# Unread products in float32r instead of bf16 in layer 2's second edge pass

## The reference

```
for i in range(2):
    x1 = gat_layer(x1, src, dst, W[i], a_s[i], a_d[i], concat = (i == 0))
    x2 = gcn_layer(x2, src, dst, edge_weight, gcn_W[i])
out = maximum(x1, x2)
# gat: per head e = leaky_relu(es[src] + ed[dst]); att = softmax of e over the edges
#      of one dst; out = sum over edges of att * Wh[src]
# gcn: sum over edges of w / deg[dst] * h[src]
```

## Time and profile before

| | us |
|---|---|
| median of 3 runs | 2940.66 |
| lowest, highest | 2939.59, 2948.7 |
| span of the profiled execution | 3321.3 |

### The profile page before, as it was taken

The page is one execution under the profiler, slowest core; times in us unless marked ns, Lnnn a source line. Parts: engine busy times, 40 slices in busy tenths (PEclk is TensorE's granted clock), DMA queues, the critical chain, the costliest instruction groups (busy, mean ns, idle before and its releaser), DMA issues.

```text
span 3321.3 us, 56445 instructions
## 1 busy us (share of the span) xinstructions
PE 2643.0 (80%) x15058; PEld 1980.1 (60%) x15146; DVE 1663.3 (50%) x6677; ACT 980.3 (30%) x4757; POOL 1410.3 (42%) x1667
## 2 busy tenths in 40 slices
PE   2444545598448888889499998989699999999998
PEld 1444444455337787778367776767566666666665
DVE  4555555597334555554244545444854444444442
ACT  2444555465212333333123333333800000000000
POOL 3666666300156666661445656660232222222210
PEclk9999999999655555555695667677899999999999
DMA  2111111163233333331423333332610000000001
GB/s 77 44 44 45 44 45 44 44 227 114 79 82 91 89 92 92 91 89 46 106 70 83 90 84 90 89 89 59 231 59 18 17 18 18 18 17 18 17 28 42
DMA packets 183897, 227.24 MB, mean 68 GB/s; under 512 B 62447, under 2 KB 146488, under 8 KB 182808
## 3 DMA queue, kind: packets, MB, share of 16 engines
q0 software_dynamic: 50176, 131.74, 14.8%
q1 hardware_dynamic: 122654, 86.45, 8.3%
q10 hardware_dynamic: 10746, 5.37, 0.6%
HBM read 183.92 MB, written 39.48 MB: 67 GB/s over the span
## 4 chain that ended last, share of the span: by engine, by line
PE 62%; DVE 10%; issue 9%; another core or an unknown queue 5%; ACT 3%; ACTq 2%; DMA 2%; SPq 0%; DVEq 0%; POOL 0%; POOLq 0%
PE banks L2510 26%; PE banks L1538 7%; PE banks L1599 4%; PE banks L1596 3%; PE banks L1597 3%; PE banks L1602 2%; PE banks L748 2%; PE banks L1600 2%; DMA arena<-dst_flat 2%; PE banks L537 1%; PE banks L540 1%; DVE arena L524 1%; PE banks L1554 1%; PE banks L2521 1%
## 5 line engine op out<-in xcount | busy, mean ns | idle before, releaser
L2510 PE MATMUL banks<-arena 128*128 128x384 bf16 (+1 forms) x5475 | 879.8, 324 | 0.0
L2510 PEld LDWEIGHTS banks<-arena 128*128 128x128 bf16 x5475 | 535.7, 98 | 341.7
L222 POOL DMA_INDIRECT arena<-value_table,arena x392 | 396.4, 1011 | 487.2 <-DMA ed_table<-arena 267.0
L222 POOL DMA_INDIRECT arena<-gat_table,arena x392 | 389.7, 994 | 347.1 <-PE banks L1602 169.0
L222 POOL DMA_INDIRECT arena<-h_table,arena x392 | 371.8, 948 | 218.0 <-PE banks L540 90.9
L537 PE MATMUL banks<-arena 128*128 128x425 bf16 x392 | 201.8, 515 | 310.2 <-DVE arena L524 179.6
L2493 POOL TENSOR_TENSOR arena<-arena 128x128 f32<-128x128 f32 x225 | 103.3, 459 | 647.5 <-DVE arena L2567 638.2
L2561 DVE TENSOR_REDUCE arena<-banks 128x128 f32<-128x384 f32 x225 | 125.3, 557 | 364.3 <-PE banks L2510 356.7
L1538 PE MATMUL banks<-arena 128*128 128x512 bf16 (+1 forms) x902 | 279.3, 406 | 17.6 <-issue 15.3
L2551 ACT ACTIVATE arena<-arena 128x128 bf16<-128x128 f32 (+1 forms) x200 | 61.9, 309 | 732.4 <-DVE arena L2567 732.4
L1596 PE MATMUL banks<-arena 128*128 128x17 f32 x784 | 227.6, 371 | 43.3 <-issue 27.2
(11 more groups left out here) (282 smaller groups left out, 4601.6 us busy)
## 6 DMA issues: line engine op xcount, KB each, us to landing
adj_rows<-arena SPq DMA_DIRECT2D x1, 20000.0 KB, 54.6
arena<-adj_rows SPq DMA_DIRECT2D x2, 7200.0 KB, 22.0
arena<-h_rows SPq DMA_DIRECT2D x225, 64.0 KB, 1.8
arena<-ed_table SPq DMA_DIRECT2D x784, 0.5 KB
arena<-h_table,arena POOLq DMA_INDIRECT x392
arena<-value_table,arena POOLq DMA_INDIRECT x392
arena<-gat_table,arena POOLq DMA_INDIRECT x392
arena<-adj_rows SPq DMA_DIRECT2D x2, 1600.0 KB, 6.2
```

What stands on the lines that cost most here:

```text
L222: return e.indirect_dma_start(into, None, table, bass.IndirectOffsetOnAxis(ap=index.bitcast(U32), axis=0))
L2510: x = e.matmul(acc[:, 0:w], C[:, sb, db * P:(db + 1) * P], old[:, sb, 0:w], start=(sb == 0), stop=(sb == LAST))
```

## The change

Pass 2 alone changes, in four places.

1. A buffer `spare` of 320 float32r columns is allocated at word 52864 of the arena, the big SBUF buffer (its 53200 words end 16 behind it).
2. In pass 2 DVE copies the first 320 columns of `wide` into it, between its two memsets, and waits for the copy before it goes on to the second memset.
3. PE waits for `e2_zero` to reach 2 before its first unread product, besides `t_made`.
4. The unread products multiply `spare[:, 128:256]` (the identity, now float32r, the stationary operand) with `spare[:, 0:n]`. Their numbers and widths become 38 of 320 at the start (24 of 512 before), five of 320 in each of the first 53 slots (three of 512), and two of 320 after each chunk (one of 512 and one of 256). That is 38 + 265 + 784 = 1087 products.

```diff
+F32R = mybir.dt.float32r
...
+        arena_at = -(-nc.sbuf_base // 32) * 32
...
+            if i:
+                spare = nc.alloc_sbuf_tensor_at("spare", [P, 320], F32R, offset=arena_at + 4 * 52864)
...
                 e.memset(acc[:, :, N + 1:NP], 0.0)
+                if i:
+                    dve_own.do(e.tensor_copy(spare[:, :], wide[:, 0:320]))
+                    dve_own.settle(e)
                 e.memset(SACC[:, N + 1:NP], 0.0).then_inc(e2_zero, 1)
...
                     e.wait_ge(t_made, 1)
-                spare = wide.bitcast(BF16)[:, 0:512]
+                    e.wait_ge(e2_zero, 2)
...
-                            e.matmul(banks[:, 7, 0:n], identb, spare[:, 0:n], start=True, stop=True, skip_group_check=True)
-
-                busy(*[512] * 24)
+                            e.matmul(banks[:, 7, 0:n], spare[:, P:2 * P], spare[:, 0:n], start=True, stop=True, skip_group_check=True)
+
+                busy(*[320] * 38)
...
-                            busy(512, 512, 512)
+                            busy(320, 320, 320, 320, 320)
                         if c is not None:
                             sums(c)
-                            busy(512, 256)
+                            busy(320, 320)
```

## The result

| | us, median | ratio to before, 95% interval |
|---|---|---|
| before | 2944.68 | |
| changed | 3129.42 | 1.0624, 1.0582 to 1.0667 |

The direction and the main term were forecast (2998 us, the clock lost), the size was not: 185 us instead of 57, outside the range of 2865 to 3055. Two later executions, one of the changed kernel (e10) and one of a variant of it (e11), took 3195 and 3196 us at a mean clock of 0.783, and are left out of the ratios.

The account below looks back on a forecast made before the run. PE was taken to bound pass 2 at half clock, its clock level deciding. Terms 80 - 17 + 2 = +65 us, scaled by 0.885 to +57, gave 2998 us; range 2865 to 3055.

Parts of the forecast that it names:

- The float32r column: Unread products on PE: one cycle a column as in bf16, 320 columns taking 0.267 us at half clock, 0.133 at full.
- R3: Rival, chance 0.10: float32r streams slower than bf16; net -46 us at two cycles a column, +200 at four.
- R1: Rival, chance 0.22: float32r products hold pass 2's clock up, 60 to 110 us faster, about 2860 us.
- The copy, the wait and the opening: Start of pass 2: copy and wait counted 0 (1.2 us at worst), the opening's extra columns +2 us.
- The stall that I counted on: 47.8 us of the chain right behind pass 2's start, made by no engine's work, expected to hide the later start.
- The weight load: PE, float32r load behind L1602, a chunk's last matmul: may show 0 to 0.07 us more at half clock.
- 17 us less: PE's time at half clock over the 360 chunks after the opening: 0.046 us a chunk saved by the shorter pair.
- R2: Rival, chance 0.14: no net effect on the clock level, only shorter pairs, 5 to 25 us less, 2925 us.
- R4: Rival, chance 0.06: nothing to be seen, lost clock rises and shorter pairs cancelling, 2940 us.
- The level: Pass 2's granted clock: fewer unread columns make rises rare; four fifths of 100 us, +80, the largest term.
- The scale to the median: Whole sum: +65 us on the profiled 3321.3 us span, times 0.885 for the unprofiled median, giving +57.
- The sign that was given: Pass 2: clock under 0.60 over 1725:2275, plain chunk 1.49 to 1.57 us at half clock, POOL's wait above 127 us.

Follow-up runs that it names:

- e10: The changed kernel run once more, on a chip where the kernel before takes 2945 us: 3135 us, 1.0611 of the kernel before.
- e11: Changed kernel with one float32r and then one bf16 product of 320 columns after each chunk, on a 2945 us chip: 1.0633 of the kernel before.
- e7: Changed kernel with float32r products of 512 and 256 columns after each chunk, the old column count: 1.0571 of the kernel before, 185 us.
- e5: Changed kernel with the start and first 53 slots in bf16 as before, float32r products only after the chunks: 1.0431 of the kernel before, 140 us.
- e12: Kernel before without any unread product in pass 2, on a 2945 us chip: 1.0013 of the kernel before.

## Why the prediction was right in kind and wrong in size

- **The float32r column** was right: one cycle a column (0.267 us behind a wide product at half clock), the bf16 end of my bounds. R3 is out, and so is R1: the clock is 0.50 and not up. The copy, the wait and the opening (+2 us) were right within what can be told on 3300 chips. The stall that I counted on to hide the start isn't in the changed kernel's trace, so on a 2945 chip a few us of them may show; that wasn't measured.
- **The weight load** is the first mis-sized term. I had "0 to 0.07 us more", taken as half, from f32 pairs that are partly hidden themselves. The pair was to go from 0.614 to 0.533 and cost a little of that; it went to 0.70 us. So "17 us less" was in truth 0.08 us a plain chunk more at half clock (1.65 against 1.57), 22 us over the 270 chunks at that clock. The exposed load was also what kept the clock from coming back (e7 against the kernel before, both with 768 columns), which I hadn't counted at all. R2 and R4 fell with it.
- **The level** was the right mechanism, mis-sized. I took four fifths of 100 us because "some rises may stay" as the shorter pair packs the chunks. That is what the bf16 version shows (a rise after each of its falls). With the load exposed there was none.
- **The scale to the median** was the step that failed most. I scaled +65 by 0.885, to +57, and so the level term in it from 80 to 71, in the belief that a faster execution makes the loss smaller, though I had written that the price of half clock is PE's own and that full-clock chunks could be cheaper. On a 3300 chip e5 measured +140, and on a 2945 chip the change +185. The first, against my unscaled +65, is nearly covered by the two terms above: all of the 100 instead of four fifths, and some 27 us more for the chunks instead of 17 less. The second isn't, and the rest is the level term again: of the 176 us of 270 chunks, 22 are the load, and about 154 the level, where scaling left me 71 (an estimate, since it takes 1.30 us a chunk for the kernel before).
- **What there was to lose.** Each run's record has its mean granted clock c, and (2c - 1) x T is its time at full clock: (2 x 0.866 - 1) x 2946 = 2157 us before, (2 x 0.804 - 1) x 3133 = 1905 changed, (2 x 0.793 - 1) x 2953.5 = 1731 with no unread products. So the kernel before has some 426 us of full clock in pass 2 and its start on a 2945 chip, and the change leaves 174 of them. (Where a trace exists the sum fits: 189 us by it for the changed kernel's profiled execution, 191 in the trace.) The rest of the program takes 3135 - 700 = 2435 us in e10 and 2960 - 522 = 2438 in e12, which leaves about 510 us for pass 2 before, 1.30 a chunk, as in the changed kernel's stretch at full clock. The change makes it 686 to 700. On a 3300 chip pass 2 is 597 to 626 us before: its clock falls 15 to 17 times in each of the five traces of it, so there is less to lose. That reading rests on sums and on the runs' clocks, not on a trace of the kernel before.
- **The sign that was given**: a clock under 0.60 over the stretch that starts 50 us behind the first chunk (0.59 in 1460:2069, of which the first 109 us are still at 1.00), and POOL's wait up from 127 to over 200 us, were both seen. "The plain chunk at 1.49 to 1.57" was not: 1.65.
- **The two rules.** PE is busy for 526.5 of 526.5 us at 0.50. The Trainium skill (TensorE: Matmul & The Clock Gate, Part 1) says that the gate follows how busy PE is. If the profile's busy row is meant, this trace contradicts it again. 320 float32r columns take 0.267 us at half clock, one cycle each, where f32 takes four. The Trainium skill (FP8 and Floating Point Precision, TensorE Precision Notes) says of the reduced kind of FP32 only that it truncates what it reads, and gives four passes to true FP32. The four cycles agree with it; the one cycle of float32r is this case's measurement.

## What to carry to other kernels

Before scaling a sum from a profiled execution to a median that is 11% lower, ask whether the clock does the same in both: a loss that consists in losing the full clock is larger, not smaller, where the full clock is held longer. Don't judge a filler by its number of columns: 768 float32r columns after each chunk lost for good a clock that came back 15 to 17 times with 768 bf16 ones. Look on the timeline at what stands ahead of a weight load of four-byte operands; behind a narrow matmul it cost 0.16 us here, behind a wide one nothing. And test the filler against nothing at all: the ones after each chunk cost 0.7% on one kind of chip, and all of them together earned nothing on the other.

## What was not expected of the hardware

- The same program takes 2945 us on some chips and 3291 to 3319 on others, and the difference shows in the stages with indirect DMAs (PE busy 291 against 199 us in 100:500, gathers at the same pitch of 1.25 us when nothing holds them). The cause was not looked for.
- A float32r product of 320 columns has a pitch of 0.267 us at half clock and 0.147 at full behind another wide one, but 0.43 and 0.25 behind a matmul of 17 columns. A bf16 one hides its load in both places (0.51 us for a pair at half clock), and an f32 matmul behind the narrow one shows the same 0.16 us as float32r.
- In the changed kernel the granted clock fell at 1568.9 us, when PE had been busy for 7.9 of the last 8.9 us, and stayed down for 526 us of unbroken matmuls.
